# A graph network on one core: the two gather stages over the edges written out turn by turn

## The reference, cut to what matters

```python
# layer 0, heads of 64
score[e] = (q[dst[e]] * k[src[e], type[e]]).sum(-1)
p[e] = softmax of score over the edges with equal dst
agg[n] = segment_sum(p[e] * v[src[e], type[e]], dst)
# layer 1, 64 features; in the kernel beside it: a linear attention over all nodes
s1[n] = segment_sum(y1[src[e]], dst)
# later: the same sum with 2 features, norms, dense layers, 8 experts per node
```

## Time and profile before

| | |
|---|---|
| median of 3 runs | 8494.61 us (8423.9 to 8496.62) |
| span of the profiled execution | 8571.6 us, its only time on record |
| `attention_edges` | 858 to 3532 us |
| `gcn_edges_and_mix1` | 4247 to 6833 us |
| PE, DVE, ACT, POOL busy | 61%, 53%, 38%, 45% of the span |
| DMA | 1154.93 MB, 135 GB/s on the mean |

### The profile page before, as it was taken

How to read it: one execution, slowest core, us unless ns; L and a number is a source line. 1 busy time by engine, 2 the same in 40 slices (tenths; PEclk the granted TensorE clock), 3 DMA queues, 4 the chain that set the end, 5 groups by cost and what they waited for, 6 DMA issues and landing times. The chain is left out here.

```text
span 8571.6 us, 116878 instructions
## 1 busy us (share of the span) xinstructions
PE 5243.7 (61%) x30143; PEld 3895.7 (45%) x30144; DVE 4536.6 (53%) x8737; ACT 3218.8 (38%) x7600; POOL 3872.1 (45%) x3841
## 2 busy tenths in 40 slices
PE   2999577777776677456623334332222247699999
PEld 2554455555555555346512212121111136588888
DVE  5555677777777777543423333343333389843333
ACT  0554566666666666311200000010000057543333
POOL 1221566666666666342366666676666413200000
PEclk7999899999999999788756666655555579789999
DMA  5554777777777777551322222222222468710000
GB/s 141 208 211 175 228 211 212 210 212 210 212 210 212 212 211 210 142 162 48 115 55 64 64 61 66 61 83 73 78 73 74 83 196 282 233 42 14 13 12 12
DMA packets 539832, 1154.93 MB, mean 135 GB/s; under 512 B 121739, under 2 KB 273458, under 8 KB 532798
## 3 DMA queue, kind: packets, MB, share of 16 engines
q0 software_dynamic: 217216, 691.51, 28.1%
q1 hardware_dynamic: 299864, 438.79, 16.0%
q10 hardware_dynamic: 22480, 21.44, 0.8%
HBM read 878.85 MB, written 280.36 MB: 135 GB/s over the span
## 5 line engine op out<-in xcount | busy, mean ns | idle before, releaser
L2231 POOL DMA_INDIRECT g_row<-y_parts,g_index x1664 | 1677.9, 1008 | 886.8 <-issue 666.8
L965 POOL DMA_INDIRECT ae_kv<-edge_table,ae_index x1664 | 1607.4, 966 | 1042.2 <-PE psum L1183 451.3
L1183 PE MATMUL psum<-ae_kv,ae_edge_hot 128*128 128x266 f32 x3328 | 882.4, 410 | 451.1 <-ACT ae_step_sums L1073 279.7
L1152 PE MATMUL psum<-ae_q,ae_node_hot 128*128 x3328 | 923.4, 440 | 75.0 <-DMA ae_q<-queries 50.4
L1183 PEld LDWEIGHTS psum<-ae_kv,ae_edge_hot 128*128 128x128 f32 x3328 | 617.7, 195 | 690.4 <-ACT ae_step_sums L1073 365.0
L2254 PE MATMUL psum<-g_row,g_keep 128*128 128x64 bf16 x4992 | 312.2, 218 | 862.3 <-issue 688.6
L1152 PEld LDWEIGHTS psum<-ae_q,ae_node_hot 128*128 128x128 f32 x3328 | 720.1, 221 | 217.2 <-issue 95.0
L1007 DVE TENSOR_TENSOR ae_kv<-ae_kv,psum 128x2048 f32<-128x2048 f32 x208 | 475.9, 2288 | 630.8 <-remote 591.3
L2427 DVE TENSOR_TENSOR g_acc<-g_acc,g_step_sums 128x64 f32 x832 | 188.0, 226 | 919.6 <-issue 699.7
L2254 PEld LDWEIGHTS psum<-g_row,g_keep 128*128 128x128 bf16 x4992 | 247.2, 114 | 926.3 <-issue 781.0
L3144 ACT ACTIVATE em_h<-psum,experts_affine 128x256 f32<-128x256 f32 (+1 forms) x800 | 404.9, 556 | 610.5 <-PE psum L3101 431.5
(11 more groups left out here) (595 smaller groups left out, 10358.9 us busy)
## 6 DMA issues: line engine op xcount, KB each, us to landing
ae_node_hot<-rel_rows SPq DMA_DIRECT2D x208, 512.0 KB
edge_hots<-g_keep SPq DMA_DIRECT2D x208, 356.0 KB
gn_hots<-edge_hots SPq DMA_DIRECT2D x208, 356.0 KB
gn_row<-source_places SPq DMA_DIRECT2D x208, 256.0 KB
ae_kv<-edge_table,ae_index POOLq DMA_INDIRECT x1664
g_row<-y_parts,g_index POOLq DMA_INDIRECT x1664
pair_sums<-gn_out SPq DMA_DIRECT2D x624, 4.0 KB
x_sorted<-nt_x SPq DMA_DIRECT2D x52, 128.0 KB
```

The costliest lines, as they stand in the source:

```text
L965: g.indirect_dma_start(out=kv[:, s, n, :], out_offset=None, in_=dram["table"], in_offset=bass.IndirectOffsetOnAxis(ap=index[:, s, n:n + 1] ...
L1152: ins = t.matmul(bank[n // 2][:, (n % 2) * D:(n % 2 + 1) * D], oht[:, s, n * P:(n + 1) * P], qb[:, bass.ds(at[n // 2], 1), :].rearrange("p ...
L1183: ins = t.matmul(bank[4 + m % 2][:, 0:CW], ohs[:, n, :], kv[:, s, n, KC:2 * D], start=n % 2 == 0, stop=n % 2 == 1)
L2231: g.indirect_dma_start(out=row[:, m, n, :], out_offset=None, in_=table, in_offset=bass.IndirectOffsetOnAxis(ap=index[:, m, n:n + 1].bitcas ...
```

## The change: no loops in the two stages

`in_turns` becomes `each_turn`, a loop of Python that writes out every turn; the loops on DVE, POOL and SP become Python ranges in the same way. The parts, their order on each engine, the buffers and the DMAs stay. With the index known when the program is built, each wait compares with a constant and each address that depends on the turn alone is a constant. The places in the accumulators are still read from a table in the program, and still take register arithmetic. Line numbers behind `in_turns` move up by 11 (by 13 behind line 2235).

```diff
--- before.py
+++ after.py
@@ -94,25 +94,14 @@
         eng.wait_ge(sem, count)
 
 
-def in_turns(eng, groups, slots, parts, peeled=1):
-
+def each_turn(groups, slots, parts):
 
     most = max(ahead for ahead, _ in parts)
     least = min(ahead for ahead, _ in parts)
-    assert most <= slots and least >= -slots and groups % slots == 0
-
-    def written_out(turns):
-        for k in turns:
-            for ahead, part in parts:
-                if 0 <= k + ahead < groups:
-                    part((k + ahead) // slots, (k + ahead) % slots)
-
-    written_out(range(-most, peeled * slots))
-    with eng.Fori(peeled, groups // slots - 1) as i:
-        for s in range(slots):
-            for ahead, part in parts:
-                part(i + (s + ahead) // slots, (s + ahead) % slots)
-    written_out(range(groups - slots, groups - least))
+    for k in range(-most, groups - least):
+        for ahead, part in parts:
+            if 0 <= k + ahead < groups:
+                part((k + ahead) // slots, (k + ahead) % slots)
 
 
 def index_tables(nc, sem, bank, c, dram, src, dst, etype, ntype):
@@ -952,7 +941,7 @@
                     wait_count(sp, col_ready, CHUNK * n)
                     wait_count(sp, index_ready, CHUNK * n)
                     chunk_load(n + 1)
-                with sp.Fori(first + 1, first + CHUNK // SLOTS) as i:
+                for i in range(first + 1, first + CHUNK // SLOTS):
                     rows(i)
             sp.wait_ge(sum_added, GROUPS * PACK)
             for a, b in ((0, 112), (112, BW)):
@@ -970,7 +959,7 @@
                 g.wait_ge(index_ready, s + 1)
                 for n in range(G):
                     gather(0, s, n)
-            with g.Fori(1, ITER) as i:
+            for i in range(1, ITER):
                 for s in range(SLOTS):
                     g.wait_ge(index_ready, i * SLOTS + s + 1)
                     for n in range(G):
@@ -1053,7 +1042,7 @@
             turn(-1, SLOTS - 1, True, False, False)
             for s in range(SLOTS):
                 turn(0, s, True, True, s > 0)
-            with v.Fori(1, ITER - 1) as i:
+            for i in range(1, ITER - 1):
                 for s in range(SLOTS):
                     turn(i, s, True, True, True)
             for s in range(SLOTS):
@@ -1133,7 +1122,7 @@
                              ).then_inc(node_hot[s], 1)
 
             a.wait_ge(place_ready, 1)
-            in_turns(a, GROUPS, SLOTS, ((-1, copy), (0, exponents), (-1, store), (0, places), (1, columns), (1, mark), (4, indices), (3, nodes)))
+            each_turn(GROUPS, SLOTS, ((-1, copy), (0, exponents), (-1, store), (0, places), (1, columns), (1, mark), (4, indices), (3, nodes)))
             a.wait_ge(carry_stored, GROUPS * 16)
 
         @block.tensor
@@ -1187,7 +1176,7 @@
 
             t.wait_ge(q_in, 16 * NB)
             t.wait_ge(packed_ready, 1)
-            in_turns(t, GROUPS, SLOTS, ((2, look_up), (0, turn), (-1, total), (0, turn_back), (2, expand)))
+            each_turn(GROUPS, SLOTS, ((2, look_up), (0, turn), (-1, total), (0, turn_back), (2, expand)))
 
 BIG = float(1 << 24)
 TOP = NB * BW - 1
@@ -2188,10 +2177,10 @@
                               of_pairs(part) if part in in_pairs else of_tiles(part))
                              for ahead, part in parts)
 
-            in_turns(eng, PHASE, 4, placed(first, 0))
+            each_turn(PHASE, 4, placed(first, 0))
             if between is not None:
                 between()
-            in_turns(eng, PHASE, 4, placed(second, PHASE // 4))
+            each_turn(PHASE, 4, placed(second, PHASE // 4))
 
         @block.sync
         def _(sp):
@@ -2206,7 +2195,7 @@
             sp.dma_start(b_out[:], w["b_out"].unsqueeze(0)).then_inc(w_in, 16)
             for n, a in enumerate((w["w_norm2"], w["bd"])):
                 sp.dma_start(vec[:, n, :], a.unsqueeze(0).broadcast_to([P, D])).then_inc(w_in, 16)
-            with sp.Fori(0, GROUPS // S) as i:
+            for i in range(GROUPS // S):
                 for m in range(S):
                     sp.wait_ge(hot_made[m], i + 1)
                     sp.wait_ge(tile_hot[m], i + 1)
@@ -2233,9 +2222,7 @@
                                              ap=index[:, m, n:n + 1].bitcast(U32), axis=0)).then_inc(gathered[m], 16)
 
             g.iota(node[:], pattern=[[P, NT]], base=0, channel_multiplier=1).then_inc(iota_made, 1)
-            for m in range(S):
-                gather(0, m)
-            with g.Fori(1, GROUPS // S) as i:
+            for i in range(GROUPS // S):
                 for m in range(S):
                     gather(i, m)
```

## The result

The kernel before takes 8494.88 us (median of 20 executions, 8423.90 to 8514.34), the changed kernel 8423.95 us (median of 20, 8405.92 to 8452.52). The ratio is 0.9933, with a 95% interval of 0.9917 to 0.9950: 71 us less by the medians, where 121 were forecast and 85 would have counted as faster. The ratio is not the quotient of the two medians, which would be 0.9917; taken at its word it is 57 us (42 to 71). The time lies inside the forecast's range; the saving is 0.59 of the forecast one by the medians and 0.47 by the ratio. And it holds for chips on which before takes 8.46 to 8.49 ms. My runs also came to chips on which it takes 7.64 ms, and there the same change costs 1.2%. One of the eight executions of before_again took 8763.61 us, the others 7632 to 7641, and it is counted in no ratio.

The account below looks back on a forecast made before the run. No engine was taken as full: DVE-PE waits bound attention, DVE's progress the second stage. Terms -10 - 13 - 73 - 25 + 0 = -121 us gave 8451 us profiled, 8374 us on the median; 8 in 10 range 8200 to 8510.

Parts of the forecast that it names:

- What bounds the kernel: No engine full: attention stage bound by a circle of waits between DVE and PE, second stage by DVE's progress.
- Attention, -10: Attention stage: without counts and branches each turn is 0.05 us shorter, over 204 turns 10 us; bounds 0 and -20.
- Second stage, first half, -13: Second stage's first-half loop: 8 groups fall from 95.9 to 94.8 us, 1.1 us times 12, 13 us saved.
- Second half, -73: Second stage's second-half loop: no code refetch at DVE's jump, 103.9 to 94.8 us per 8 groups, 73 us saved.
- the stretch at 96.0 us: Second stage's second half: gathers read as the loop's first pass before any jump back, taken as evidence for the refetch.
- Fewer instructions on DVE, -25: Second stage: DVE's lists lose counts and addresses (310 to 224, 344 to 248), 1 us per 8 groups, 25 us saved.
- Longer code, +0: Both stages: bringing in the longer code costs nothing, PE's idle time covering its stops; bounds 0 and +128 us.
- code at the wrong moment: Rival, both stages: engines run out of held code every few turns, PE's 110 stops of 1.16 us cost +128; chance 0.12.
- POOL's floor: Rival, second stage: fewer DVE instructions let POOL run through its gathers, halfway -250 us, 8025 to 8245; chance 0.13.
- carried over, 8374: Whole kernel: the -121 us, 8451 us on the profiled 8571.6 us execution, transferred to the runs' median of 8494.61 us.

Follow-up runs that it names:

- before_again: The kernel before, unchanged, run again on a faster chip: 7638.61 us, ratio 0.9996.
- before_third: The kernel before, unchanged, run once more on a slower chip for a second profile: 8462.25 us, ratio 1.0006.
- split_after: Changed kernel with DVE's 128 x 1024 comparison in the second stage split into eight of 128 x 128: ratio 0.9964 to the kernel before (8483.37 us).
- dve_loops: Kernel before with all loops written out except DVE's three: ratio 0.9944 to the kernel before (8483.37 us).
- dve1_loops: Kernel before with all loops written out except DVE's in the attention stage and the second stage's first half: ratio 0.9918 (before 8462.25 us).
- dve2_only: Kernel before with only DVE's loop in the second stage's second half written out: 8418.72 us, ratio 0.9937.
- dve_single: Kernel before with each pass of DVE's loops, both stages, as its own single-pass loop, counts kept in registers: ratio 0.9934 (before 8483.37 us).
- dve1_loops_again: Kernel before, all written out except DVE's loops in attention and the second stage's first half, on a faster chip: 0.67% slower, ratio 1.0067.

## Why the prediction was wrong

**What bounds the kernel** was right for the chip of the profile, and only for it. On the faster chips POOL is the bound of both stages in the same program.

**Attention, -10.** Not there. Between two like profiles (before_third and after) the stage went from 2647 to 2658 us, +11. The usual turn did get shorter (12.35 to 12.25), and the long turns behind the uneven places took it back (14.7 for 12.4 us, 15 times). The 12.49 us of the earlier trace rows belonged to that one execution, whose stage was 27 us longer. The loss shows only with all five engines written out: 192 turns take 2391 us in before_third, 2403 in the changed kernel and 2396 in split_after, but 2384 and 2383 in dve_loops and dve1_loops, which keep DVE's loop there. These are single profiles.

**Second stage, first half, -13.** The size came: 1145 us for 96 groups in before_third, 1132 after. But dve_loops and dve1_loops, which are alike up to there, differ by 10 us in it (1132 and 1142), so it is hardly clear of chance.

**Second half, -73.** Right in its place and size: 1104 to 1025 us between those two profiles, 79, with the 1026 of dve2_only saying that this one loop is all of it. Its cause was not shown. I took the refetch at the jump for it; with the refetch in place dve_loops runs at 94.4. And the sign that I read for it was misread: the stretch at 96.0 us, 5770 to 5866, is not "the first pass of the loop, before it turned back once". DVE had turned back at 5765 already, its first pass began at 5655, within the stretch that I took as written out, and the pass without a jump before it was the slowest, 109.7 us. What both cures have in common is that the beat does not set in; why it does in before stays open.

**Fewer instructions on DVE, -25.** Oversized. dve_single keeps them and is 3 us longer in the second half than dve2_only, and no longer in the first (1142 and 1143 us, with the first half's loop not written out in dve2_only).

**Longer code, +0.** Nearly so: the +11 us of the attention stage are its only sign. The rival "code at the wrong moment" had +128 for it, ten times as much, and on PE, where the stops that showed are ACT's. "POOL's floor" did not come on these chips, and on the faster ones it was reached before the change.

**The steps that failed are two terms of the sum, "Attention, -10" and "Fewer instructions, -25", and then "carried over, 8374".** Between before_third and the changed kernel's profile, the nearest that I have to a like pair, the span fell by 94 us (8513.5 to 8419.7), where the sum says 121. The attention stage gave +11 for -10, the counts on DVE some -3 for -25, and the second half and the rest gave back some 16. Then I took the whole saving off the median, as if each execution had it. It was read on an execution of 8571.6 us, longer than all twenty timed ones (8514.34 at most), to which the execution after (8419.7) was even -152; before_third's, 8515.1 us as timed, was the longest of its eight. Between the medians it is -71. What the middle executions of before lack is not known. It is not shown to be the beat: in the eight passes from the third on the two profiles differ by 16 us (834 and 818) of their 58. The spread of before's three times, 8424 to 8497, stood in front of me, and I used it as noise of the measurement, not as a sign that something in the kernel comes and goes.

**The other sign.** The slower rival was given 0.12 for fetch stops. On the faster chips the change is slower by 1.2% through a mechanism that I did not list: a gather waits for a DVE instruction with two inputs in SBUF, and written-out code moves these instructions against the gathers. That the forecast had even the sign was luck of the chip: on three of the five chips of the experiments it would have been wrong.

## What to carry to other kernels

If the execution that was profiled is longer than all the timed ones, set a saving against that execution, and take a second profile before carrying it over to the median. Read a loop's passes from the engine whose loop it is, not from one that runs ahead. Write loops out one at a time: here one of thirteen carried the gain and others carried a loss. Where POOL issues gathers without a pause, the moment at which DVE's instructions with two SBUF inputs begin decides their length, and an edit on other engines can move it (dve1_loops_again).

## What the hardware showed that I had not expected

- Two levels between chips: the same program in 7638 and in 8460 to 8490 us, with attention turns of 10.03 and 12.45 us on the mean and DMA at 265 and 213 GB/s in them. Their cause is open.
- Steps of about 1.4 us from one matmul of 0.2 us to the next in the second stage, on the slower chips only. Their cause is open.
- A gather that starts while a DVE instruction with two inputs in SBUF runs ends 0.82 us after it, up to 1.96 us long instead of 0.945 in the lines above.
- Bringing in a loop's code again, five packets and 2.7 to 3.2 us of DVE's time per iteration, was hidden on the faster chips (with that loop kept and all others written out the ratio is 1.0121, with all written out 1.0122) and did not keep dve_loops from its gain on a slower one.
